# TensorE's three blocks of a batch in another order, and VectorE's additions split around its small sums

## The reference, cut to what matters

```python
# x (64, 128, 2048) f32; weights (16, 128, 128); A (64 adapters, 2048, 16); B (64 adapters, 16, 2048)
W = weights[condition]                        # one 128x128 matrix for each of 64 batches
x = x + einsum('bct,bcd->bdt', x, W)          # mixes the 128 channels
Bx  = einsum('bni,bri->bnr', x, B[adapter])   # 2048 -> 16, for each channel
out = x + einsum('bnr,bor->bno', Bx, A[adapter])   # 16 -> 2048, scaling 1
```

## Time and profile before

| | |
|---|---|
| Timed runs | 398.72 us median of 3 (398.45 to 399.15) |
| Profiled execution, its own time | 398.63 us |
| Its span, first to last instruction | 396.8 us |
| TensorE matmul busy | 380.9 us (96%) |
| VectorE busy | 271.3 us (68%) |
| ScalarE busy | 221.5 us (56%) |
| Mean granted TensorE clock | 0.989 |
| Moved between HBM and SBUF | 152.37 MB, mean 384 GB/s |

### The profile page before, as it was taken

The page is one execution under the profiler, slowest core; times in us unless marked ns, Lnnn a source line. Parts: engine busy times, 40 slices in busy tenths (PEclk is TensorE's granted clock), DMA queues, the critical chain, the costliest instruction groups (busy, mean ns, idle before and its releaser), DMA issues.

```text
span 396.8 us, 16443 instructions
## 1 busy us (share of the span) xinstructions
PE 380.9 (96%) x6164; PEld 351.2 (89%) x6164; DVE 271.3 (68%) x576; ACT 221.5 (56%) x513; POOL 29.7 (7%) x71
## 2 busy tenths in 40 slices
PE   7899999999999999999999999999999999999970
PEld 7889999999999999999999999999999999999960
DVE  0267767766866766776776686686677677678683
ACT  2566555556555555655555655555565565565540
POOL 1200000000000000000000000000000000000000
PEclk9999999999999999999999999999999999999995
DMA  6999999999999999999999999999999999999528
GB/s 222 417 416 413 404 403 411 400 400 386 418 388 402 404 396 419 385 413 395 401 409 394 415 390 402 408 391 407 405 402 396 415 395 399 408 402 371 235 121 304
DMA packets 29103, 152.37 MB, mean 384 GB/s; under 512 B 3233, under 2 KB 3490, under 8 KB 12962
## 3 DMA queue, kind: packets, MB, share of 16 engines
q1 hardware_dynamic: 29090, 152.19, 96.8%
HBM read 85.07 MB, written 67.11 MB: 384 GB/s over the span
## 4 chain that ended last, share of the span: by engine, by line
PE 91%; DMA 3%; DVE 2%; SPq 1%; issue 1%; ACT 0%; DVEq 0%
PE f_bank L333 58%; PE low_bank L368 17%; PE z_bank L347 16%; DMA ab_in<-in_lora 2%; DVE x_out L262 1%; DVE z_pair L288 0%; DMA ids<-in_ids 0%; SPq L138 0%; DVE z_all L293 0%; SPq L125 0%; SPq L128 0%; SPq L139 0%; DVE at L280 0%; DVEq L53 0%; ACT ft L220 0%
## 5 line engine op out<-in xcount | busy, mean ns | idle before, releaser
L333 PE MATMUL f_bank<-m_sel,x_in 128*128 128x128 f32 x2048 | 246.1, 278 | 2.4 <-ACT ft L220 1.4
L333 PEld LDWEIGHTS f_bank<-m_sel,x_in 128*128 128x128 f32 x2048 | 233.6, 192 | 10.6 <-issue 1.4
L220 ACT COPY ft<-f_bank 128x512 f32<-128x512 f32 x256 | 149.6, 585 | 78.4 <-PE f_bank L333 77.5
L262 DVE TENSOR_TENSOR x_out<-low_bank,ft 128x512 f32<-128x512 f32 x252 | 156.5, 682 | 2.0
L288 DVE TENSOR_TENSOR z_pair<-z_bank,z_two 16x128 f32<-16x128 f32 x128 | 36.8, 287 | 92.8 <-ACT z_two L228 90.8
L368 PE MATMUL low_bank<-z_all,at 16*128 16x128 f32 x2016 | 75.1, 283 | 2.1 <-DVE x_out L262 2.1
L368 PEld LDWEIGHTS low_bank<-z_all,at 16*128 16x128 f32 x2016 | 62.9, 186 | 15.4 <-issue 15.4
L347 PE MATMUL z_bank<-ft,ab_in 128*16 128x128 f32 x2048 | 68.3, 274 | 0.0
L236 ACT COPY z_all<-z_all 16x128 f32<-16x128 f32 x128 | 37.8, 296 | 50.1 <-DVE z_all L293 48.6
L280 DVE STREAM_TRANSPOSE at<-ab_in 128x512 f32<-128x512 f32 x64 | 44.8, 700 | 19.1 <-DMA ab_in<-in_lora 19.1
L347 PEld LDWEIGHTS z_bank<-ft,ab_in 128*16 128x16 f32 x2048 | 50.3, 96 | 7.8 <-issue 0.2
(11 more groups left out here) (9 smaller groups left out, 2.6 us busy)
## 6 DMA issues: line engine op xcount, KB each, us to landing
x_in<-in_x SPq DMA_DIRECT2D x63, 1024.0 KB, 9.2
out<-x_out SPq DMA_DIRECT2D x62, 1024.0 KB, 7.3
ab_in<-in_lora SPq DMA_DIRECT2D x64, 256.0 KB, 8.1
out<-x_out SPq DMA_DIRECT2D x8, 256.0 KB, 4.4
w_all<-in_weights SPq DMA_DIRECT2D x1, 1024.0 KB, 7.3
x_in<-in_x SPq DMA_DIRECT2D x1, 768.0 KB, 4.6
x_in<-in_x SPq DMA_DIRECT2D x1, 256.0 KB, 3.1
w_first<-in_weights SPq DMA_DIRECT2D x2, 64.0 KB, 4.1
```

The costliest lines, as they stand in the source:

```text
L220: nc.scalar.copy(ft[k][u][:], f_bank[BANK_OF[u]][:]).then_inc(copied, 1)
L262: nc.vector.tensor_tensor(x_out[k][:, UNIT * u:UNIT * (u + 1)], banks_of(b)[u][:], ft[k][u][:], ALU.add).then_inc(added, 1)
L333: last = nc.tensor.matmul(f_bank[BANK_OF[u]][:, P * c:P * (c + 1)], x_in[k][:, UNIT * u + P * c:UNIT * u + P * (c + 1)], m_sel[k][:], star ...
```

## The change

In a slot TensorE runs the low rank of b-1 before z of b, where it ran z first. VectorE adds the first two units of b-1 ahead of `sum_tiles` of b and the other two behind it. The last turn's unrolled code follows the same pattern, and the low rank of batch 62, which now stands before z of batch 63, gets a wait for all copies, because it writes into `f_bank`s. ScalarE, GpSimd and SyncE keep their code. No instruction is added or removed apart from waits.

```diff
             def turn(q, last):
                 for k in range(BODY - 2 if last else BODY):
                     b = BODY * q + k
+                    if begun(b - 1):
+                        add_units((k - 1) % BODY, range(UNITS // 2), b - 1, q - (k == 0))
                     sum_tiles(k, b)
                     if begun(b - 1):
-                        add_units((k - 1) % BODY, range(UNITS), b - 1, q - (k == 0))
+                        add_units((k - 1) % BODY, range(UNITS // 2, UNITS), b - 1, q - (k == 0))
                     turn_a((k + 2) % BODY, b + 2, q + (k + 2) // BODY + 1)
...
             turn(TURNS - 1, True)
+            add_units(BODY - 3, LATE[0:2], BATCHES - 3, TURNS - 1)
             sum_tiles(BODY - 2, BATCHES - 2)
-            add_units(BODY - 3, LATE[0:2], BATCHES - 3, TURNS - 1)
+            add_units(BODY - 3, LATE[2:], BATCHES - 3, TURNS - 1)
             sum_tiles(BODY - 1, BATCHES - 1)
-            add_units(BODY - 3, LATE[2:], BATCHES - 3, TURNS - 1)
             add_units(BODY - 2, range(UNITS), BATCHES - 2, TURNS - 1)
             add_units(BODY - 1, range(UNITS), BATCHES - 1, TURNS - 1)
...
                 if isinstance(b, int) and b == BATCHES - 2:
                     pe.wait_ge(added, UNITS * (b - 1) + 1)
+                    pe.wait_ge(copied, UNITS * BATCHES)
...
-                    sum_z(k, b, q + 1)
                     if begun(b - 1):
                         add_low_rank((k - 1) % BODY, b - 1)
+                    sum_z(k, b, q + 1)
                 if last:
                     add_low_rank(BODY - 1, BATCHES - 1)
```

## The result

The changed kernel takes 405.46 us (median of 4 runs, 404.94 to 406.12) against 398.72 us: a ratio of 1.0172, 95% interval 1.0159 to 1.0184. It is slower by 6.7 us; the forecast was 405.5. The profiled execution took 405.94 us with a span of 404.1 us, 7.3 us more than before.

The account below looks back on a forecast made before the run. TensorE's 5.87 us cycle was taken to set the pace, with the DMA engines just keeping up. Loop stalls of 6.7 us plus 0.2 at the end made 6.9 us, 405.5 us forecast; range 400.5 to 411.5.

Parts of the forecast that it names:

- TensorE's blocks: TensorE's switches between kinds of block: new ones cost 0.31 us like the others, so nothing, 0.05 us a slot either way.
- The rival with a cheap switch: TensorE's mix to low rank switch nearly free: 0.20 us gained a slot, 12 us in all, 393.5 us; chance 0.06.
- The chain: In a loop slot, VectorE's adds, z_pair, place_z, then ScalarE's copy of unit 0 at 2.12 us after mix start.
- the 7.8 us that I gave for this rule: Loop loss if VectorE holds z_pair until the adds finish, at mix start + 0.53, instead of 6.7 us.
- The stall: Unit 3 of mix waits for unit 0's copy: 0.08 us in three slots of four, 0.24 in the fourth; 6.7 us.
- The step on the unrolled slots: In the six or so unrolled slots z_two comes 0.07 us earlier and the copy step takes 0.64: no stall.
- The end: After the last mix: last add 1.55 us later, store lag can go; +0.2 us taken, bounds -0.3 and +0.7.
- What I said the profile would show: Signs after: some 56 f_bank waits for ft of 0.05 to 0.3 us, cycle near 5.99, last add near 1.55 us later.

Follow-up runs that it names:

- the first experiment: The changed kernel with ScalarE copying unit 0 of the next mix before it places z: 398.75 us, ratio 1.0003 against the kernel before.
- The doses: The changed kernel with one more small ScalarE copy behind place_z: 425.29 us; the changed kernel with mix unit 3 in unit 1's bank: 435.76 us.

## Why the prediction was right

- **TensorE's blocks.** The two new switches, from the last weight load of a block to the first of the next: mix to low rank, 226.41 + 3.73 - 0.19 = 229.95 to 230.26, 0.31 us. Low rank to z, 230.26 + 0.79 = 231.05 to 231.36, 0.31. Both as the rows of the other switches said. One of those rows was not clean: z straight to mix in the earlier trace rows stood before a load of x that came last. In the changed loop that switch measures 0.31 too (225.41 + 0.79 - 0.10 = 226.10 to 226.41). The rival with a cheap switch is out, here and by the first experiment. The Trainium skill (TensorEngine Tiling (Array Packing), Tiling Modes) says that a change of tiling mode drains TensorE; the equal gaps agree with a cost at each change, and no run tells whether a drain is the cause.
- **The chain.** Forecast after mix start: adds -0.89 to -0.79, z_pair 0.51, place_z 1.46 and 1.62, unit 0's copy 2.12. Measured: -0.79 (-0.86 in the fourth slot), 0.53, 1.48 and 1.62, 2.12 (2.25 in the fourth slot). z_pair stands 0.03 behind the adds in three slots of four, as the rule on held instructions in the Trainium skill (VectorE: DVE Perf Modes, Two Vector instructions with no wait between them) has it. This put 0.02 on the chain, and the step from place_z to the copy gave it back (0.64 where I took 0.66), so the 7.8 us that I gave for this rule did not come.
- **The stall.** 0.08 us as forecast, in the fourth slot 0.21 instead of 0.24: 5.95 x 3 + 6.08 = 23.93 us a turn against 23.48, 0.45 x 14 = 6.3 us in the loop (6.7 forecast). The last mix is 6.4 us later. The doses show that it is this wait and that it has no slack. The step on the unrolled slots failed at the end of the kernel: I had no stall there, because z_two comes 0.07 us earlier. It does (382.02, the last mix's start + 0.14), but z_pair stands behind the adds (382.41, + 0.53), so nothing is won, and each of the last three mixes is 0.08 us longer, 0.24 us in all. In the first turn it is 0.01 us.
- **The end.** This term of the sum was mis-sized: +0.9 in the profiled execution where I had +0.2, outside the +0.7 I gave as a bound. Taken apart, the last add ends 18.3 us after the last mix starts instead of 15.1 (3.2 later, I had 1.55). The last store's issue ends 0.36 us behind it instead of 2.19 (I had read the lag of the stores before as 1.5 us; against this 0.36 it was 1.8). From there to the end it is 3.6 us instead of 4.0. My times held the gap: z of 62 at 380.33, low rank of 62 not before 383.45. What they did not hold is that the clock falls behind it. With the gap filled the last add ends at 16.9 and the end is 0.1 us shorter than before, inside my bounds.
- **Where the two sums met.** The profiled execution lost 6.4 + 0.9 = 7.3 us where I had 6.9. The four timed runs are 404.94, 404.97, 405.94 and 406.12, and the median of 405.46 lies in the empty middle between two pairs. So the closeness of 405.5 to 405.46 is luck; the mechanism and the 6 us of the loop are not.
- **What I said the profile would show** was wrong in two points: no 56 waits for ft are listed, and the last add is 3.2 us later and not 1.55.

## What to carry to other kernels

An engine that runs in program order makes everything behind a late instruction late, urgent or not: before an order is changed, list for each engine which of its instructions has the nearest deadline, and put that one first. Here one line of ScalarE's program (the copy that frees a bank ahead of the copy that nobody needs for almost 2 us) was worth the whole loss of the loop. A cycle with no visible wait can still have little or no slack somewhere. Measure slack as deadline minus arrival, from start times, because a stall of 0.1 us showed in no list of waits here.

## What the runs showed of the hardware that was not expected

- TensorE's granted clock fell from 1.00 (2.4 GHz) to 0.50 (1.2 GHz) within 1 us of its resuming after 2.24 us without matmuls, and z of batch 63 took 1.91 us instead of 1.07. In two other kernels with this gap it fell later: some 1.7 us after resuming in the one with ScalarE's order changed (mean 0.65 from 384 to 386 us, resumed at 382.94; z of 63 took 1.42 us), some 1.6 us in the one with only the last turn changed (mean 0.85 from 384 to 386 us, resumed at 383.84; 1.52 us). With 16 records of matmuls in the gap, whose result nobody uses, it stayed at 1.00 through the same stretch. What sets the moment no run shows.
- Runs of the kernels with this gap spread with their mean clock. With ScalarE's order changed, four are at 397.7 to 397.9 us with 0.991, two at 398.05 and 398.49 with 0.985 and 0.984, and six at 399.0 to 399.6 with 0.981 to 0.982.
- A delay of 0.08 or 0.21 us does not appear as a wait in the lists. One of 0.39 us does, as 0.31, and one of 1.08 us, as 1.00.
- Eight stores of 256 KB took 6.35 and 6.36 us to issue with the issue of a 1 MB store ending 0.26 us before, 4.97 and 4.96 us with it ending 1.66 us before; their last issue ended 2.0 to 2.2 and 0.8 us behind the last add. In the changed kernel (4.86 us) and in the one with the gap filled (4.51 us) it ended 0.36 us behind the last add, so there the adds set the length.
